# A fused attention and FP4 feed-forward block: the weighted sums of a tile in two lots, and another order of all engines

## What is computed

```python
xn = layernorm(x)                                   # per row, eps 1e-5
q, k, v = xn @ Wq.T, xn @ Wk.T, xn @ Wv.T           # 16 heads of 16; q and k are divided by their L2 norm
attn = softmax(q @ k.T + bias)                      # bias: 0 <= key - query < 128 only, minus slope * distance
s = (attn @ v) @ Wo.T
gate, up = fp4(xn) @ fp4(w_gate).T, fp4(xn) @ fp4(w_up).T     # 704 columns each
g = silu(fp4(silu(gate) * up) @ fp4(w_down).T)      # fp4: blocks of 16 on the E2M1 grid, times a scale
out = x + s * g
```

## Time and profile before

| | us |
|---|---|
| median of 3 runs | 560.42 (557.68 to 562.02) |
| the profiled execution | 557.35 |
| its span | 555.5 |
| from `hidden(2)` to `hidden(29)`, 27 tiles | 420.7 |
| PE busy in the span | 450.9 (81%) |
| POOL, DVE, ACT busy | 378.5, 379.5, 366.5 |

### The profile page before, as it was taken

The page is one execution under the profiler, slowest core; times in us unless marked ns, Lnnn a source line. Parts: engine busy times, 40 slices in busy tenths (PEclk is TensorE's granted clock), DMA queues, the critical chain, the costliest instruction groups (busy, mean ns, idle before and its releaser), DMA issues.

```text
span 555.5 us, 21323 instructions
## 1 busy us (share of the span) xinstructions
PE 450.9 (81%) x8612; PEld 323.0 (58%) x8612; DVE 379.5 (68%) x776; ACT 366.5 (66%) x559; POOL 378.5 (68%) x854
## 2 busy tenths in 40 slices
PE   0247779997889888998889897788999887889995
PEld 0125546665656566676666665565766565666773
DVE  4899888885776644776775864576677654666663
ACT  4458878875776555777665865666777655766750
POOL 4754668886776666788775876775788766775443
PEclk9978999998999877999997998889999988989998
DMA  8223127656755326555563543564565424555434
GB/s 303 60 48 58 36 43 131 111 84 92 133 114 112 68 48 113 113 114 114 113 114 68 115 96 64 114 112 82 110 120 118 88 47 92 104 104 96 104 49 108
DMA packets 175010, 54.40 MB, mean 98 GB/s; under 512 B 164224, under 2 KB 174272, under 8 KB 174912
## 3 DMA queue, kind: packets, MB, share of 16 engines
q1 hardware_dynamic: 174480, 52.90, 48.1%
q10 hardware_dynamic: 432, 0.13, 0.1%
HBM read 7.54 MB, written 4.19 MB: 21 GB/s over the span
## 4 chain that ended last, share of the span: by engine, by line
issue 24%; PE 22%; POOL 20%; DVE 14%; DMA 13%; SPq 3%; ACT 3%; POOLq 1%; DVEq 0%; ACTq 0%
DMA qk_slots<-qk_stack 9%; PE bank_b L597 8%; PE up L372 6%; SPq L1842 2%; DVE up L800 2%; DVE h_amax L783 2%; PE scores L517 2%; POOL ah_stack L1554 2%; POOL x_stack L1507 2%; DMA ahT<-ah_stack 2%; POOL x_stack L1514 1%; POOL x_stack L1519 1%; PE gt L560 1%; DMA x_all<-wproj 1%; POOL rsq L1615 1%
## 5 line engine op out<-in xcount | busy, mean ns | idle before, releaser
L1309 ACT ACTIVATE probs<-scores 128x768 f32<-128x768 f32 (+1 forms) x101 | 80.4, 796 | 58.5 <-PE scores L541 53.2
L597 PE MATMUL bank_b<-probs,vals 64*32 64x64 f32 (+1 forms) x3904 | 79.5, 234 | 17.1 <-issue 14.5
L776 DVE SCALAR_TENSOR_TENSOR up<-up,h_gain,gate 128x704 f32<-128x704 f32 x31 | 29.7, 958 | 90.6 <-PE up L372 90.6
L597 PEld LDWEIGHTS bank_b<-probs,vals 64*32 64x32 f32 (+1 forms) x3904 | 66.6, 117 | 27.6 <-issue 18.4
L372 PE MATMUL up<-wgu_hi,xT 128*128 128x352 f16 x248 | 70.6, 353 | 1.4 <-issue 1.0
L372 PE MATMUL gt<-wgu_hi,xT 128*128 128x352 f16 x256 | 62.4, 312 | 2.1 <-DVE y L917 1.8
L1519 POOL TENSOR_TENSOR x_stack<-x_ring,x_stack 128x256 f16<-128x256 f32 x32 | 21.4, 669 | 58.1 <-ACT x_stack L1172 58.1
L517 PE MATMUL scores<-hidden_keys,neg 64*64 64x256 f16 x404 | 32.0, 307 | 35.0 <-DMA qk_slots<-qk_stack 30.4
L873 DVE TENSOR_TENSOR bank_q<-bank_q,rsq 128x512 f32<-128x512 f32 x32 | 22.4, 699 | 50.5 <-POOL rsq L1647 50.5
L372 PE MATMUL bank_q<-wproj_hi,xT 128*128 128x512 f16 x128 | 45.2, 395 | 11.0 <-DMA xT<-x_stack 11.0
L1172 ACT ACTIVATE pv_t<-bank_b 128x512 f32<-128x512 f32 x31 | 18.5, 597 | 47.2 <-PE bank_b L597 47.1
(11 more groups left out here) (231 smaller groups left out, 1414.3 us busy)
## 6 DMA issues: line engine op xcount, KB each, us to landing
out<-y SPq DMA_DIRECT2D x32, 128.0 KB, 2.7
x_all<-x SPq DMA_DIRECT2D x20, 128.0 KB, 3.9
x_all<-x SPq DMA_DIRECT2D x3, 512.0 KB, 4.3
x_all<-wproj SPq DMA_DIRECT2D x1, 768.0 KB, 7.3
dn_raw<-wd SPq DMA_DIRECT2D x1, 704.0 KB, 9.0
probs<-wg SPq DMA_DIRECT2D x1, 640.0 KB, 5.6
probs<-wu SPq DMA_DIRECT2D x1, 640.0 KB, 7.9
xT<-x_stack SPq DMA_TRANSPOSE x34, 3.3
```

The lines of the kernel that those rows point to most:

```text
L597: done = e.matmul(pv_bank(i)[32 * n:32 * n + 32, grp * P + q:grp * P + q + HB], va, pr, start=first and grp == 0, stop=last and grp == 3)
L776: e.scalar_tensor_tensor(up_of(t), up_of(t), h_gain[:], gate_of(t), ALU.mult, ALU.mult).then_inc(s_h, 1)
L1309: e.activation(probs[j % P_BUFS][:, grp, :, window(j)].rearrange("p (b e) w -> p b e w", b=2), score_banks(j, grp)[:, :, :, window(j)], AC ...
```

## The change

The function `weigh` is taken out of `pv`, and `pv` ends after half of its matmuls (in the program 32 of 64, in the records 64 of 128). The other half is a new step, `pv_rest`, which stands behind `up_mm_last` in the loop. `wo_mm` goes from behind `scores(t - 1, 3)` to a place between `pv` and `scores(t - 1, 2)`, `v_mm` from before `scores(t - 1, 0)` to behind it, and `back` between the halves of `down_mm`. `gate_mm` is written at the start of the next iteration and stays where it was, between `qk_mm` and `scores`. The lists of DVE, ACT, POOL and SP are in another order too, before, in and after the loop. No instruction of the loop is added or taken away. Core of the diff, with the loops of PE and SP and the parts of the others that are spoken of below:

```diff
+            def weigh(i, t, part, block, rows, q, first=False, last=False):
...
                 if not final(i):
-                    weigh(i + 1, 1, "both", slice(0, HB), 0, first=True).then_inc(s_pv_prev, 1)
-                weigh(i, 0, "own", slice(0, P), 0, first=final(i))
+                    weigh(i, i + 1, 1, "both", slice(0, HB), 0, first=True).then_inc(s_pv_prev, 1)
+                weigh(i, i, 0, "own", slice(0, P), 0, first=final(i))
+
+            def pv_rest(i):
                 if not final(i):
-                    weigh(i + 1, 1, "prev", slice(0, P), HB)
+                    weigh(i, i + 1, 1, "prev", slice(0, P), HB)
                     e.wait_ge(s_pv_prev, i + 1 - i // TPB)
-                weigh(i, 0, "both", slice(HB, P), HB, last=True).then_inc(s_pv, 1)
+                weigh(i, i, 0, "both", slice(HB, P), HB, last=True).then_inc(s_pv, 1)
...
             for t in range(4, 31):
+                gate_mm(t - 2)
                 scores(t - 1, 0)
+                v_mm(t)
                 scores(t - 1, 1)
                 pv(t - 3)
+                wo_mm(t - 4)
                 scores(t - 1, 2)
                 up_mm(t - 2)
                 up_mm_last(t - 2)
-                back(t - 3)
+                pv_rest(t - 3)
                 scores(t - 1, 3)
-                wo_mm(t - 4)
                 down_mm(t - 4, 0, 4)
+                back(t - 3)
                 down_mm(t - 4, 4, FT)
                 qk_mm(t + 1)
-                gate_mm(t - 1)
-                v_mm(t + 1)
...
                 hidden(t - 2)
-                lo_qk(t)
                 amax_h(t - 2)
                 wide_h(t - 2)
-                denom(t - 3)
+                lo_qk(t)
                 rscale_h(t - 2)
+                denom(t - 3)
                 norm_h(t - 2)
                 gated(t - 4)
-                if exists(t + 2):
-                    wide_x(t + 2)
                 attend(t - 3)
...
             for t in range(8, 31):
-                store(t - 6)
-                ah_transpose(t - 3)
-                if exists(t - 9) and exists(t - 9 + X_RING):
-                    refill(t - 9)
+                stack_transpose(t + 1)
+                ah_transpose(t - 2)
+                if exists(t - 8) and exists(t - 8 + X_RING):
+                    refill(t - 8)
+                store(t - 5)
                 x_transpose(t + 3)
-                stack_transpose(t + 1)
```

More of the change, by code:

```diff
@@ L576, in wo_mm @@
                 done.then_inc(s_wo_mm, 1)
+            def weigh(i, t, part, block, rows, q, first=False, last=False):
+                for grp in range(4):
+                    for n in range(GRP):
+                        e_, b_ = divmod(n, 2)
+                        pr = probs[t % P_BUFS][rows, grp, b_ * 2 + e_, blk(t, block)]
+                        va = vals[rows, t % V_SLOTS, part, grp * GRP + n, :]
+                        done = e.matmul(pv_bank(i)[32 * n:32 * n + 32, grp * P + q:grp * P + q + HB], va, pr,
+                                        start=first and grp == 0, stop=last and grp == 3)
+                return done
             def pv(i):
@@ L644, in tensor_program @@
             tr_wd(1)
+            sub_wd(0)
             scores(1, 3)
-            sub_wd(0)
+            sub_wd(1)
             tr_wd(2)
-            sub_wd(1)
             qk_mm(3)
-            scores(2, 0)
             gate_mm(1)
             up_mm(1)
+            v_mm(3)
+            scores(2, 0)
             up_mm_last(1)
-            v_mm(3)
+            pv(0)
+            pv_rest(0)
             scores(2, 1)
+            back(0)
             scores(2, 2)
-            pv(0)
             scores(2, 3)
-            back(0)
             qk_mm(4)
-            gate_mm(2)
-            v_mm(4)
             for t in range(4, 31):
+                gate_mm(t - 2)
                 scores(t - 1, 0)
+                v_mm(t)
                 scores(t - 1, 1)
                 pv(t - 3)
+                wo_mm(t - 4)
                 scores(t - 1, 2)
@@ L669, in tensor_program @@
                 up_mm_last(t - 2)
+                pv_rest(t - 3)
+                scores(t - 1, 3)
+                down_mm(t - 4, 0, 4)
                 back(t - 3)
-                scores(t - 1, 3)
-                wo_mm(t - 4)
-                down_mm(t - 4, 0, 4)
                 down_mm(t - 4, 4, FT)
                 qk_mm(t + 1)
-                gate_mm(t - 1)
-                v_mm(t + 1)
+            gate_mm(TILES - 3)
             scores(TILES - 2, 0)
+            v_mm(TILES - 1)
             up_mm(TILES - 3)
@@ L1037, in vector_program @@
-            ln_stats(4)
             norm_w(6)
             norm_w(7)
+            wide_x(2)
+            lo_qk(1)
             values(1)
-            ln_moments(4)
-            amax_x(2)
-            up_x(1)
             round_w(6)
             squares(2)
+            up_x(1)
             grid_x(1)
+            values(2)
+            rscale_x(2)
             round_w(7)
-            values(2)
+            ln_stats(5)
             hidden(0)
-            wide_x(2)
+            ln_moments(5)
+            norm_x(2)
@@ L1065, in vector_program @@
+            norm_x(3)
             squares(3)
-            up_x(2)
-            grid_h(0)
-            grid_x(2)
-            rscale_x(3)
-            ln_moments(6)
-            norm_x(3)
-            lo_wo()
             lo_wd(2)
+            values(3)
+            hidden(1)
+            amax_h(1)
             amax_x(4)
-            hidden(1)
-            values(3)
-            amax_h(1)
             unit(3)
             wide_h(1)
+            denom(0)
+            ln_moments(6)
+            attend(0)
@@ L1080, in vector_program @@
+            rscale_h(1)
+            lo_qk(3)
+            lo_wo()
+            norm_h(1)
             wide_x(4)
             up_x(3)
-            rscale_h(1)
             grid_x(3)
             rscale_x(4)
-            lo_qk(3)
-            norm_h(1)
-            denom(0)
-            attend(0)
-            up_h(1)
             norm_x(4)
             squares(4)
+            up_h(1)
+            values(4)
             grid_h(1)
-            values(4)
+            ln_stats(7)
             up_x(4)
-            ln_stats(7)
@@ L1716, in gpsimd_program @@
             root(2, ROOT)
-            lo_qx(1)
             lo_xn(3)
             fine_x(2)
+            hi_qx(2)
             x_norm(4)
-            pad_dn()
+            ones(3)
             coarse_h(0)
```

411 lines of the change are left out of this document (204 added, 207 removed).

## The result

The changed kernel takes 535.92 us (532.24 to 538.59, 4 runs) where the kernel before takes 560.75 us (557.68 to 562.02, 4 runs). The ratio is 0.9628, with a 95% interval from 0.9562 to 0.9693: faster by 3.7%. The prediction was 540 us, with a range from 512 to 565.

What follows compares the result with a forecast made beforehand. PE was taken to set a floor of 13.2 us a tile, with about 2.4 us of disturbances. 14.10 + 0.10 + 0.26 + 0.37 = 14.83 us against 15.58, 20 us less over 27 tiles: 540 us, range 512 to 565.

Steps and rivals of the forecast that it cites:

- What the stops are, and the two lots: PE's weighted sums: idling blamed on late program pieces; splitting the sums cuts 0.54 us a tile to 0.10.
- some 4 us: PE's program: how late a fetch comes when it falls together with a DMA transpose.
- The SP queue: `stack_transpose` no longer waits behind `x_transpose`: PE's 1.13 us a tile of q and k transpose waits go, down to 0.1.
- U: Start of the PE slot after the up product, the zero point for times in a tile; 235.42 us in the good tile.
- The round through `ahT`: `wo_mm` moved up waits for its transposed input: 6.86 + 4.1 + 0.07 + 2.87 us at best, 14.10 taken as tile time.
- the best case: Tile time of 13.90 us if the `ahT` transpose lands in 4.1 us, as when the queues are quiet.
- Late landings and the clock: Loop disturbances: late `ahT` transposes at 0.26 us a tile, PE's lower clock in 5 tiles at 0.37.
- `v_mm` behind the first scores: PE waits 0.3 to 0.7 us a tile for `values` at the first lot, free while `wo_mm` waits longer for `ahT`.
- the floor that I gave without `ahT`: Tile time without the wait for `ahT`: PE's work of 12.47 plus 0.75 us, 13.2 us; POOL and ACT fit.
- The ends of the program: Reordered start and end outside the 27 tiles, 94 and 41 us: change taken as 0, bounds 4 us either way.
- `ahT` in time: Rival: the transpose landing ahead of `wo_mm` is hidden; 13.75 us a tile, 511 us in all; chance 0.13.
- Late landings: Rival: most `ahT` transposes take 5.8 us and the clock falls; 16.4 us a tile, 582 us; chance 0.12.

## Why the prediction was right, by its steps

**What the stops are, and the two lots.** Held. The stops of 0.54 us a tile are gone, not merely 0.10 left; joining the lots brings them back, and the split takes them away in the other order too. The sum had left some out. The kernel before also has stops marked "issue" away from the sums:

```profile
PE scores L541 <- issue: 4.1, 3, 1.5
PE scores L538 <- issue: 1.6, 1, 1.6
PE up L372 <- issue: 1.0, 1, 1.0
```

With them it is 12 stops and 20.6 us in the 27 tiles, 0.76 us a tile.

That they are PE's program arriving late can be read from the traces. Number all PE instructions of the trace (matmuls, weight loads, and those of the sequencer, 17527 in all) in order of time, and cut the count into blocks of 256. The 12 stops stand at the 194th or 195th instruction of a block, each of them. So do the 11 of the kernel with joined lots, and all 58 stops in the loops of the 13 kernels traced here, wherever in a tile they fall. Each ends 1.2 to 1.6 us after the end of a 16 KB packet of the queue "q8 instruction", and each of these packets began while a DMA transpose was in flight.

What the prediction had wrong is how much of the lateness is due to the transpose. In the 12 stops PE went on 3.8 to 4.9 us after it had passed the same point of the block before; that is the "some 4 us". But the packet began 1.2 to 2.4 us after that point, and in the loop of the kernel before the middle value is 1.1 us for packets that met no transpose and 1.7 for those that met one. So the transpose adds well under 2 us. With 1.1 us, some 1.0 for the packet and 1.3 behind it a block comes after 3.4 us: by this estimate 256 instructions in 2.2 us would make PE stop for about 1 us even with no transpose near. No run shows that case, and no run changed the fetches alone.

The Trainium skill (Runtime: NRT & Kernel Launch, "Instruction fetch mechanics") calls the crossing of such a block mostly hidden. The measurement decides here: the kernel before lost 14.5 us to stops at the sums, 20.6 with the others, and the clock behind them.

**The SP queue.** The scores were to begin at U + 6.8 from data, at U + 7.15 from PE's own work; they began 7.17 us behind the second lot, and the wait is gone. The mechanism was right; how much hangs on it was not seen. Without it the changed kernel takes 595 us, and the kernel before gains 5.8% by it alone.

**The round through `ahT`.** Held, each part within 0.2 us: 6.80, 4.17 and 3.06 against 6.86, 4.1 with 0.07, and 2.87. The landing was at its best value, not between the bounds, and the stretch behind `wo_mm`'s start 0.19 us longer, so the tile took 14.03 us: between the 13.90 of the best case and the 14.10 of the forecast. That `wo_mm` gave up its 7.3 us of slack is what costs the 4.9% between this kernel and the one with `wo_mm` late (0.9628 against 0.9177).

**Late landings and the clock.** Together 0.10 + 0.26 + 0.37 = 0.73 us a tile were predicted over 14.10; measured are 14.69 less 14.03 = 0.66. Of it the clock is 13.37 less 13.12 = 0.25 (six windows at 1.1 us each; five at 2.0 were taken), and late landings and the rest are 0.41 (0.36 with the residual stops). The sum is closer than its parts, and that is luck.

**`v_mm` behind the first scores.** "It costs nothing while that holds" was right for its own kernel: the wait is 0.53 us a tile, within 0.3 to 0.7, and in the late-`wo_mm` kernel its removal moved only the kind of wait. But the floor that I gave without `ahT`, 13.2 us, was wrong. POOL and ACT were taken as fitting by their busy time (11.4 and 10.7 us); ScalarE's chain of 4.0 us between `gate_mm` and the up product is a limit of order, not of busy time, and sets 13.62.

**The ends of the program.** Taken as 0 with bounds of 4. The stretch up to `hidden(2)` grew from 94.0 to 95.6 us, the one behind `hidden(29)` from 40.8 to 44.4: 5.2 us, outside the bound. The loop gained 24.0 us, not 20; the two errors cancel by luck, and the profiled execution is 18.8 us faster (538.59 against 557.35), where 20 were predicted.

**The rivals.** `ahT` in time would have given 511 us. It did not happen, but the kernel that makes it true took 509 us, so the rival's time was well placed. Late landings were the minority: 16 of 32 took 4.1 us, eight 5.0 or more.

## What to carry to other kernels

A tuned pipeline is a set of slacks. A step that waits for a DMA and stands 7 us behind it absorbs a landing that is 1.7 us late; at 4 us each late landing is paid, and the clock after it. So an operation should move toward its input only if what it frees is worth more. Where an engine idles with nothing to wait for, count its instructions up to each stop: if the counts are the same modulo 256, it waits for its program, and its densest run is to be broken up with long instructions. And before a floor is read from busy times, follow the chain of each other engine from the result that starts it to the buffer that it frees.

## What the runs showed of the hardware

A VectorE operation can take three times as long beside a GpSimd one. `norm_x` (128x256, float32, both operands in SBUF), in the kernel before, in the changed one, and in the changed one with `norm_x` and `unit` swapped (operations by line: us, mean ns):

```profile
L756 DVE TENSOR_TENSOR x_ring<-x_ring,x_rscale 128x256 f32<-128x256 f32 x32 | 14.8, 464 | 0.0
```

```profile
L767 DVE TENSOR_TENSOR x_ring<-x_ring,x_rscale 128x256 f32<-128x256 f32 x32 | 43.9, 1371 | 0.0
```

```profile
L767 DVE TENSOR_TENSOR x_ring<-x_ring,x_rscale 128x256 f32<-128x256 f32 x32 | 15.8, 494 | 0.0
```

In the changed kernel it runs at the same time as GpSimd's `lo_h`:

```profile
246.44 1.54 DVE L767 TENSOR_TENSOR x_ring<-x_ring,x_rscale 128x256 f32<-128x256 f32 x1
...
246.32 1.38 POOL L1564 TENSOR_TENSOR ah_stack<-h_grid,h_fine 128x704 f16<-128x704 bf16 x1
```

It ends at 247.98, just behind `lo_h` at 247.70, as if it had got hardly anything done before. With the swap, `unit`, whose operand and result are in `bank_q`, overlaps `lo_h` by some 0.3 us (245.71 to 246.40 beside 246.11 in one tile) and keeps its 691 ns. VectorE's busy time falls from 414.8 to 385.7 us, and the time of the kernel does not move, since VectorE is not what it waits for.
